# Row totals of the half row that holds block C in the first sweep, and narrow strips loaded by quadrant and chunk

## What is computed

```python
# layer 1: Chebyshev terms of h = relu(layernorm(x))
terms = [h, L @ h]
for _ in range(2, 4):
    terms.append(2.0 * (L @ terms[-1]) - terms[-2])
x = x + einsum('kni,kio->no', terms, weight)
# layer 2: neighbour mean, with h = relu(layernorm(x))
deg = clip(sum(adj, axis=1) + 1.0, 1.0)
z = concat([h, (adj @ h + h) / deg]) @ W + b
out = x + relu(z) / max(norm(relu(z)), 1e-12)
```

## Time and profile before

| what | value |
|---|---|
| median of three runs | 2600.36 us (2599.3 to 2612.91) |
| profiled execution, its own time | 2599.41 us |
| span from its first to its last instruction | 2597.3 us |
| mean granted TensorE clock | 0.922 |
| PE busy | 2195.6 us, 85% |
| DVE busy | 1676.3 us, 65% |
| POOL busy | 1343.5 us, 52% |
| ACT busy | 675.7 us, 26% |
| bytes moved by DMA | 702.62 MB, mean 271 GB/s |

### The profile page before, as it was taken

How to read it: one execution, slowest core, us unless ns; L and a number is a source line. 1 busy time by engine, 2 the same in 40 slices (tenths; PEclk the granted TensorE clock), 3 DMA queues, 4 the chain that set the end, 5 groups by cost and what they waited for, 6 DMA issues and landing times.

```text
span 2597.3 us, 29224 instructions
## 1 busy us (share of the span) xinstructions
PE 2195.6 (85%) x11792; PEld 1693.0 (65%) x11792; DVE 1676.3 (65%) x1242; ACT 675.7 (26%) x1639; POOL 1343.5 (52%) x1440
## 2 busy tenths in 40 slices
PE   1888899999999769888899957898988999877776
PEld 1655667778888657677677745676766777644454
DVE  7676787758776246465566436666556877657666
ACT  3434341534322325011112425411111222000000
POOL 5566655555654344445454244444665665655551
PEclk9999999999999889988898969898989999987888
DMA  9999999999998677657687766888987999988885
GB/s 278 328 343 330 337 337 334 320 314 343 333 331 275 159 215 238 252 196 243 221 273 254 222 167 201 255 267 266 288 244 266 309 328 325 295 258 268 238 218 151
DMA packets 225097, 702.62 MB, mean 271 GB/s; under 512 B 48835, under 2 KB 79555, under 8 KB 224963
## 3 DMA queue, kind: packets, MB, share of 16 engines
q0 software_dynamic: 168192, 664.89, 77.8%
q1 hardware_dynamic: 51776, 34.64, 5.3%
q10 hardware_dynamic: 4994, 1.25, 0.4%
HBM read 698.55 MB, written 2.10 MB: 270 GB/s over the span
## 4 chain that ended last, share of the span: by engine, by line
PE 42%; DVE 7%; another core or an unknown queue 7%; issue 7%; SPq 2%; ACT 1%; DMA 0%; POOL 0%; DVEq 0%; ACTq 0%
PE ps_pair L795 31%; PE ps_single L807 6%; DVE ring L684 5%; PE ps_pair L800 3%; SPq L423 2%; PE ps_out L756 1%; PE ps_out L762 1%; ACT ring L502 1%; PE ps_out L751 0%; DMA ring<-in_adj_dram,index 0%; PE ps_out L758 0%; POOL ring L453 0%; PE ps_out L761 0%; ACT sum_p L521 0%
## 5 line engine op out<-in xcount | busy, mean ns | idle before, releaser
L453 POOL DMA_INDIRECT ring<-in_adj_dram,index x1424 | 1341.5, 942 | 1201.0 <-issue 390.5
L684 DVE STREAM_TRANSPOSE ring<-ring 128x2048 f32<-128x2048 f32 (+7 forms) x742 | 1498.2, 2063 | 580.7 <-ACT ring L502 353.0
L795 PE MATMUL ps_pair<-ring,vec 128*128 128x256 f32 x5760 | 1327.8, 389 | 86.0 <-issue 67.2
L795 PEld LDWEIGHTS ps_pair<-ring,vec 128*128 128x128 f32 x5760 | 1109.4, 195 | 294.3 <-issue 133.3
L807 PE MATMUL ps_single<-ring,vec 128*64 128x256 f32 x4528 | 628.7, 408 | 186.0 <-issue 165.7
L502 ACT ACTIVATE ring<-ring 128x1024 f32<-128x1024 f32 (+7 forms) x736 | 576.7, 787 | 451.9 <-DMA ring<-in_adj_dram,index 337.3
L807 PEld LDWEIGHTS ps_single<-ring,vec 128*64 128x64 f32 x4528 | 383.3, 146 | 404.2 <-issue 300.6
L519 ACT ACTIVATE sum_s<-ps_single 128x512 f32<-128x512 f32 x56 | 33.3, 594 | 547.8 <-PE ps_single L807 313.9
L521 ACT ACTIVATE sum_p<-ps_pair 128x512 f32<-128x512 f32 x45 | 26.7, 594 | 473.5 <-PE ps_pair L795 391.0
L502 ACT ACTIVATION_READ_ACCUMULATOR ring<-ring 128x1 f32 x736 | 138.9, 189 | 2.1 <-issue 2.1
L800 PE MATMUL ps_pair<-ring,vec 128*64 128x256 f32 x336 | 88.4, 405 | 35.5 <-DVE vec L634 25.9
(11 more groups left out here) (83 smaller groups left out, 442.4 us busy)
## 6 DMA issues: line engine op xcount, KB each, us to landing
ring<-in_adj_dram,index POOLq DMA_INDIRECT x1424
ring<-in_adj_dram SPq DMA_DIRECT2D x160, 96.0 KB
ring<-in_adj_dram SPq DMA_DIRECT2D x160, 64.0 KB
ring<-in_adj_dram SPq DMA_DIRECT2D x160, 32.0 KB
out_dram<-vec SPq DMA_DIRECT2D x64, 32.0 KB
res<-in_x_dram SPq DMA_DIRECT2D x4, 256.0 KB, 8.1
res<-in_x_dram ACTq DMA_DIRECT2D x4, 256.0 KB, 9.4
tmp<-in_L_gnn_weight_dram ACTq DMA_DIRECT2D x2, 64.0 KB
```

Of the source, the lines that this page charges most:

```text
L453: pool.indirect_dma_start(strip_of(i)[:, g, :], None, adj_q, bass.IndirectOffsetOnAxis(ap=index[:, 0:1], axis=0), element_offset=(QN * (g ...
L684: nc.vector.transpose(blocks, blocks).then_inc(s_turned, 1)
L795: last = nc.tensor.matmul(ps_pair[n % 2][:, cells], vec[:, CB * J + c, :, :], moving, start=(pair == 0), stop=(pair == pairs - 1))
```

## The change

Three things are changed.

1. `Row.summed` totals the other half in sweep 1: the one that holds block C. The remaining half of the row is totalled in sweep 2 if C is below 8 (blocks 8 to 15) and in sweep 3 otherwise (blocks 0 to 7). Two strips of a half can now hold parts of it, so `more_sums` gets two slots, and where both are used one more small addition on DVE joins them. The number of rows with later totals goes from 30 to 16. The strips with totals go from 92 to 82, and none of them is narrow.
2. A narrow strip is loaded by 8 DMAs, not 16. Each goes to one quadrant of 32 partitions. Before, a DMA took one row quarter with both chunks (32 rows x 2 pieces). Now it takes one chunk with all four row quarters (32 rows x 4 pieces). The pieces are of the same size as before, 512 bytes a block.
3. `NARROW_LOAD` goes from 9.0 to 8.0. In the planner's tables this moves two epilogues on DVE by one strip: that of sweep 1, C = 15 from behind strip 68 to behind strip 69, and that of sweep 3, C = 0 from behind strip 112 to behind strip 113. Every other entry of `end_strip` stays.

```diff
--- before.py
+++ after.py
@@ -68,7 +68,7 @@
 BLOCK_COST = (0.86, 1.72)
 SUMS = 4
 STORE_LAG = 12
-NARROW_LOAD, LANDING, COMBINE, SLACK, AHEAD = 9.0, 2.0, 4.0, 1.0, 6.0
+NARROW_LOAD, LANDING, COMBINE, SLACK, AHEAD = 8.0, 2.0, 4.0, 1.0, 6.0
 CHAIN = {1: 3.0, 2: 3.0, 3: 7.0, 4: 0.0}
 SINGLE, PAIR = 0, 1
 JOINED = 2
@@ -106,13 +106,14 @@
     def summed(self, k):
 
         _, J0, w = self.pieces[k]
-        own = NB // 2 * (self.C // (NB // 2))
+        half = NB // 2
+        lo, hi = J0, J0 + w
         if self.sweep == 1:
-            return None if J0 <= self.C < J0 + w else (J0, J0 + w)
-        if self.sweep == 2:
-            lo, hi = max(J0, self.C + 1), min(J0 + w, own + NB // 2)
-        elif self.sweep == 3:
-            lo, hi = max(J0, own), J0 + w
+            return (lo, hi) if lo <= self.C < hi else None
+        if self.sweep == 2 and self.C < half:
+            lo = max(lo, half)
+        elif self.sweep == 3 and self.C >= half:
+            hi = min(hi, half)
         else:
             return None
         return (lo, hi) if lo < hi else None
@@ -287,7 +288,7 @@
         sum_strip.append(ahead)
     end_step = [steps_to[i + 1] for i in end_strip]
 
-    adj_v = adj.rearrange("(a c r) m -> a r c m", a=Q, r=32)
+    adj_g = adj.rearrange("(a c r) m -> r c a m", a=Q, r=32)
     x_v = x.rearrange("(a c q) f -> a q c f", a=Q, q=32)
     adj_q = adj.rearrange("n (a m) -> (n a) m", a=Q)
     out_v = out.rearrange("(a c q) f -> a q c f", a=Q, q=32)
@@ -310,7 +311,7 @@
         sum_p = sb("sum_p", [P, BN])
         vec_t = sb("vec_t", [P, BN])
         row_sums = sb("row_sums", [P, NB, G])
-        more_sums = sb("more_sums", [P, SUMS, G])
+        more_sums = sb("more_sums", [P, SUMS, 2, G])
         rdeg = sb("rdeg", [P, CH])
         ident = sb("ident", [P, P])
         fold = sb("fold", [P, 32])
@@ -358,7 +359,7 @@
 
             if narrow[i]:
                 k = narrow_strips.index(i)
-                return s_narrow[k % NSEM], 16 * Q * Q * (k // NSEM + 1)
+                return s_narrow[k % NSEM], 16 * Q * (CB // H) * (k // NSEM + 1)
             k = wide_strips.index(i)
             return s_wide[k % NSEM][p], 16 * 2 * (k // NSEM + 1)
 
@@ -417,11 +418,11 @@
                 if free_at[i] > 0:
                     sp.wait_ge(s_unit, free_at[i])
                 at = CB * rows[n].C + CB // H * h
-                for ar in range(Q):
+                for c in range(CB // H):
                     for a in (0, 2, 1, 3):
                         col = a * QN + J0 * UC
-                        sp.dma_start(strip_of(i)[32 * a:32 * a + 32, ar:GH:Q, :],
-                                     adj_v[ar, :, at:at + CB // H, col:col + w * UC])\
+                        sp.dma_start(strip_of(i)[32 * a:32 * a + 32, Q * c:Q * c + Q, :],
+                                     adj_g[:, at + c, :, col:col + w * UC])\
                             .then_inc(s_narrow[narrow_strips.index(i) % NSEM], 16)
             for n, C in finished[stored:]:
                 store_row(n, C)
@@ -494,7 +495,8 @@
                     lo, hi = row.summed(i - first_strip[n])
                     if row.sweep > 1 and extra_rows.index(n) >= SUMS:
                         act.wait_ge(s_degsum, extra_rows.index(n) - SUMS + 1)
-                    into = row_sums[:, row.C, :] if row.sweep == 1 else more_sums[:, extra_rows.index(n) % SUMS, :]
+                    into = row_sums[:, row.C, :] if row.sweep == 1 else \
+                        more_sums[:, extra_rows.index(n) % SUMS, sums_of(n).index(i) // H, :]
                     for p in range(steps_of[i]):
                         act.wait_ge(*loads_of(i, p))
                         for g in range(GH)[groups_of(i, p)]:
@@ -612,7 +614,10 @@
                     dve.wait_ge(s_row, n)
                 if n in extra_rows:
                     dve.wait_ge(s_summed, sums_to[sum_strips.index(sums_of(n)[-1]) + 1])
-                    nc.vector.tensor_tensor(row_sums[:, C, :], row_sums[:, C, :], more_sums[:, extra_rows.index(n) % SUMS, :],
+                    more = more_sums[:, extra_rows.index(n) % SUMS, :, :]
+                    if len(sums_of(n)) > H:
+                        then(nc.vector.tensor_tensor(more[:, 0, :], more[:, 0, :], more[:, 1, :], ALU.add))
+                    nc.vector.tensor_tensor(row_sums[:, C, :], row_sums[:, C, :], more[:, 0, :],
                                             ALU.add).then_inc(s_degsum, 1)
                 if row.sweep == 1:
 
```

## The result

The changed kernel takes 2588.53 us (median of 5 runs, 2586.5 to 2605.74) against 2601.87 us for the kernel before (5 runs on the same chip, 2599.3 to 2612.91). The ratio is 0.9944, with a 95% interval of 0.9921 to 0.9967, so the gain is 13.3 us by the medians, and lies between 8.6 and 20.6 us (2601.87 us times one less the two bounds).

A forecast was written before the change was run, and what follows sets the result against it. Transfers were taken to bound most of sweep 1, PE most of the rest, short rows waiting on each other. Terms -12 - 4 + 4 - 2 = -14 us from 2599.4 gave 2585.4, forecast 2586 us; 2560 to 2612 us holds 8 in 10.

The forecast's parts named there:

- the term of -12 us in sweep 1: Sweep 1, 66 to 573 us: epilogues start earlier, transfers gain 12 us, bounds 0 and 29 us.
- its own test ("if the sweep 1 window keeps its 330 GB/s"): Sweep 1 window, 66 to 573 us: the forecast is wrong if its transfer rate stays at 330 GB/s.
- the first rival: Sweep 1 and strip 145: transfers or PE's pace eat the gain, 2600 us; chance 0.20.
- Totals at the end of sweep 2, -4 us: End of sweep 2: evacuation no longer waits for strip 112's totals, nor combination for its turn; 4 us gained.
- Totals moved within sweep 2, +4 us: Strips 81 and 82: totals now stand between transfer and turn, 2.5 and 1.5 us, together 4 us lost.
- the forecast's sign of being wrong: Sweep 2: the forecast is wrong if PE's waits for DVE grow past 10 us.
- Twelve rows at 0 us, +30 without cover: Six later rows each in sweeps 2 and 3: totals of first strips are covered, 0 us; without cover 30 us.
- the slower rival: Twelve rows of sweeps 2 and 3: totals delay late strips, 2.5 us each, 2618 us; chance 0.14.
- ACT's instructions, the moved epilogues, 0 us: ACT's 80 fewer totals, 15 us of a mostly idle engine, and two epilogues moved on DVE: 0 us.
- Narrow loads, -2 us: Strips 144 and 145: half the DMAs, issue in 3.9 us, DVE freed sooner; 2 us gained, ends 0 and 17.
- its rival, transfers at half the rate: Narrow loads: four far rows in one DMA halve the rate, 10 us reach PE, 2598 us; chance 0.04.
- The stop between the sweeps, left as it is: Between sweeps 1 and 2, 900 to 926 us: cause unknown, up to 23 us either way, assumed unchanged.

The follow-up runs named there:

- Old_half_first_only: Kernel before with its totals in sweep 1 alone (old half), those of sweeps 2 and 3 left out; 2581.00 us, ratio 0.9899.
- new_half_first_only: Kernel before with totals in sweep 1 alone, of the half that holds block C, later ones left out; 2573.64 us, ratio 0.9862.
- loads_only: Kernel before with the new narrow loads (8 DMAs) alone, totals and planner as before; 2279.28 us, ratio 1.0018.
- totals_only: Kernel before with the new choice of totals alone, 16 DMAs a narrow strip and 9.0 in the planner; 2282.52 us, ratio 1.0026.
- no_totals: Kernel before without any row totals, row_sums filled with a constant; 2249.56 us, ratio 0.9878.
- new_high_rows: Changed kernel with the new choice of totals for C = 8 to 15 alone, old choice below; 2601.11 us, ratio 1.0008.
- new_low_old_loads: Changed kernel with the new choice for C below 8 only and the 16 DMAs a narrow strip of before; 2588.02 us, ratio 0.9952.
- new_low_rows: Changed kernel with the new choice of totals for C below 8 only, old choice for the rest; 2586.57 us, ratio 0.9950.
- after_plan9: Changed kernel with NARROW_LOAD at the 9.0 of before; 2290.35 us, ratio 1.0066 to the kernel before.

## Why the prediction was right, and where not

**The time and the sign** were right, the sum by luck: the term of -12 us in sweep 1, most of the -14 us, is not borne out. Between the two traces sweep 2 is shorter by 11.7 us, for which the sum held -4 and +4.

**Totals in sweep 1, -12 us: the step that failed.** Its mechanism was right up to DVE: its wait for ACT fell below 40 us, to 23.4. The step to the transfers failed. By its own test ("if the sweep 1 window keeps its 330 GB/s") it was wrong, at 327, and the DMA share stayed at 0.96 where 0.98 was forecast. DVE got the time, but the epilogue waits for PE's combination, and POOL's stops for PE stayed at 67.4 us. That is the first rival, in this stage. The end of sweep 1 (its last evacuation) came at 874.9 us before and at 878.0 us in both profiles of the changed kernel. Old_half_first_only and new_half_first_only, which differ only in the half, have 882.7 and 874.2 us. On the first chip loads_only has 825.7 us, totals_only 821.0 and no_totals 822.2, so there even leaving all totals out gives 3.5 us. The traces put the term between -8.5 and +3.1 us, executions with the same sweep 1 differ by 3.3 and 3.5 us, and its sign stays open.

**Totals at the end of sweep 2, -4 us.** Right in place and size between the two traces: ACT's totals no longer stand ahead of the evacuation, and the distance from the row before to C = 0 is 56.8 us, not 60.6. The turn of strip 112 no longer outlasts PE's combination either (by the rows it did so by 0.9 us, not 0.7). But the choice of totals is only one of two ways to this gain. new_high_rows and loads_only keep the totals of strip 112 and have the new loads, and they take 56.8 us too: ACT is done with the totals 5.5 and 4.4 us before the evacuation. In new_high_rows:

```profile
1482.87 0.60 ACT L534 ACTIVATE sum_p<-ps_pair 128x512 f32<-128x512 f32 x1 [5.52 <-PE ps_pair L811]
```

The new loads bring strip 112 sooner. DVE turns it as it lands, in new_low_old_loads 0.5 us before the evacuation (1490.18 us) and in new_low_rows, with the new loads, 9.3 us before it (1483.52 us):

```profile
1489.66 3.38 DVE L700 STREAM_TRANSPOSE ring<-ring 128x3072 f32<-128x3072 f32 x1 [5.22 <-DMA ring<-in_adj_dram]
```

```profile
1474.22 3.38 DVE L700 STREAM_TRANSPOSE ring<-ring 128x3072 f32<-128x3072 f32 x1 [3.04 <-DMA ring<-in_adj_dram]
```

**Totals moved within sweep 2, +4 us.** Right in place and about right in size. PE waits 2.6 us more at strips 81 and 82, and the rows C = 7 and 6, to which they belong, lose 1.4 to 3.2 us on the slower chips and 4.7 and 4.8 us on the first. By the forecast's sign of being wrong, PE's waits for DVE in sweep 2 past 10 us, nothing could be told: the longest was 10.64 us before already. What the sum does not have is that sweep 2 from C = 13 on is 11.7 us shorter between the two traces: 5.1 at C = 5, 5.5 at C = 2 and 3.7 at C = 0, less what other rows lose. The removed totals do not explain the first two, since new_high_rows keeps them and takes 50.4 us at C = 5 and 58.2 at C = 2, where before has 54.8 and 64.5 and after 49.7 and 59.0.

**Twelve rows at 0 us, +30 without cover.** For the six rows of sweep 2 the 0 us was right, to 0.1 us on the first chip. For the six of sweep 3 the slower rival was right in kind, at 5 to 18 us in the traces. I had read the cover at strip 93 of sweep 2 and used it for sweep 3 as well, where transfers run at 281 GB/s, beside 242 in sweep 2, and ACT waits for the strips.

**ACT's instructions, the moved epilogues, 0 us.** ACT is busy for 15.6 us less (forecast 15), without effect. For the epilogues, after_plan9 takes 7.8 us more than totals_only and carries the new loads as well; 8.0 against 9.0 alone was not run, so that stays open.

**Narrow loads, -2 us.** The issue fell as forecast, from 6.9 to 9.6 us a strip to 3.2 to 6.5 us (one of 8.3). That a strip by itself lands sooner was wrong. Strip 68 is issued from 854.7 us and free for totals at 865.09 us before; after, it is issued from 855.04 us and turned at 865.48 us, 10.4 us both times:

```profile
855.04 15.04 SPq L424 DMA_DIRECT2D ring<-in_adj_dram  x12
```

```profile
865.48 3.38 DVE L689 STREAM_TRANSPOSE ring<-ring 128x3072 f32<-128x3072 f32 x1 [11.02 <-DMA ring<-in_adj_dram]
```

Where strips stand one behind the other in SP's queue, as at strip 112, the later ones do come sooner, but by the medians that is worth nothing here. The stop at strip 145 stayed: its load is issued by 1832.1 us and lands at 1854.4, and PE works on through nearly all of it. The two comparisons of the loads alone give 4 us slower (fast chip) and 1.5 us faster within the noise. The term is 0 within the noise, and its rival, transfers at half the rate, did not come either. The page's line on queues, before and after:

```profile
q1 hardware_dynamic: 51776, 34.64, 5.3%
```

```profile
q1 hardware_dynamic: 47936, 34.62, 5.8%
```

The same bytes travel in 7% fewer packets that take 5.8% and not 5.3% of the engines' time, so each takes some 18% longer. The narrow loads are most of this queue (a strip of three blocks is 1.57 MB), and a doubled time would show as nearly double the share. The Trainium skill ("DMA: Bandwidth & Descriptors", Latency and other measured facts) has copies with a row pitch of 4 or 8 MiB at half the rate of 512 KiB; they run between HBM tensors, and the pitch is that from partition to partition. Here the four pieces of one partition lie 64 MiB apart, which the page does not cover, and the rate is not halved.

**The stop between the sweeps, left as it is.** It stayed, 24.30 us before PE's next matmul where the trace before has 24.43. What it hangs on is now shown in part: with POOL's burst held it goes. On the first chip it is absent with the burst in place. By what way the burst holds up the row is open.

**What stays open**: by what way the choice in the rows C below 8 gains its 10.8 us. It acts in sweep 1, in sweep 2 and, as totals left out, at the start of sweep 3, and no experiment parts these three. (new_low_rows has the new loads and 8.0 as well; the loads alone are worth nothing, 8.0 alone was not run.) Open too are why the trace before is long in sweep 2, and the size of the sweep 1 term.

## What to carry to other kernels

A wait that is removed is worth what the next waiter in the chain allows: before pricing it, read what else the freed engine's next instruction needs, here PE's combination. The cover at one place is no evidence for another stage; read the landing of the strips in each. Before a shorter stretch is put down to work that left it, look at a kernel without that work: here it was no shorter. And stretches of single executions scatter by 3 us and more. A gain of half a per cent is a gain of this chip until it is run on another.

## What was not expected of the hardware

- The same kernel takes 2275.5 us on one chip and 2597 to 2609 us in the three other comparisons. On the quick one the transfers reach 365 GB/s in slices where the chip of the result has 333, the mean granted clock is 0.96 against 0.92, and the stop between the sweeps is absent (in loads_only 15.4 us from C = 14 to C = 13, against 44 us in the kernel before).
- Between 906 and 931 us PE stands for 24.3 us while a burst of POOL's transfers is under way. When the burst is held, the row C = 13 ends 27 us sooner (915.06 against 942.30 us).
- The plain load of strip 68, three blocks, lands 10.4 us after its first issue, whether it is 16 DMAs or 8. That of strip 145, of the same size and with POOL's transfers beside it, lands 22 us after its last issue.
